# A graph attention layer on one core: the edge stage's pipeline one step deeper, its weighted sum one step later

## The chip, the core and the metric

The kernel runs on one core of a Trainium2 chip. The core has five engines with instruction queues of their own: TensorE (PE, matrix products and transposes through the PSUM banks), VectorE (DVE), ScalarE (ACT), GpSimd (POOL) and SyncE (SP, here DMA issues and bookkeeping). They wait for each other by semaphores. The metric is the device time of one execution in microseconds (us), median of several runs.

## The reference, cut to what matters

```python
h = relu(layer_norm(x))                         # x: 6250 rows of 256, float32
q, k, v = h @ wq + bq, h @ wk + bk, h @ wv + bv
scores = sum(q[dst] * k[src], -1) / 16 + (edge_weight * we + be)   # 200,000 edges
p = exp(scores - segment_max(scores, dst)[dst])
out = segment_sum(p * v[src], dst) / segment_sum(p, dst)           # softmax over each dst's edges
y = layer_norm(h + out + h @ ws + bs) * g1 + b1
result = x + layer_norm(y + gelu(y @ w1 + b_ff1) @ w2 + b_ff2) * g2 + b2
```

The edge list is sorted by `dst`, and `dst` is drawn as the whole part of 6250 u^2 with u uniform in 0 to 1. So the low rows have many edges and the high ones few: the share of the edges with dst below r is the square root of r / 6250.

## The kernel before

**Stages.** (1) Setup: x is normalised, q is multiplied with the key weights beforehand and kept as three bf16 parts (`q3`), the plan of the edge stage is worked out, the normalised rows h go to HBM (`h_rows`). (2) The edge stage, 440 steps. (3) A tail per block of 128 rows: product with wv, layer norm, feed-forward, layer norm, output.

**Edge stage.** The 200,000 edges are cut into 391 chunks of 512 (4 columns of 128 edges), padded to 392. The rows belong to 49 blocks of 128. A step is one pair of a chunk and a block; a chunk that reaches over a block's end takes one more step. A loop trip holds 8 steps (U), and a table `steps_tab`, made in setup, says which chunk and block each has.

For a chunk, GpSimd gathers the 512 source rows from HBM with four indirect DMAs of 128 rows (L488) into one of 8 slots of `rows`. Then, in a step:

- DVE marks by a one-hot table which edge has which row of the block (`mark`, L705), two steps ahead of its dot products, and ACT makes the matching mask (`prepare`, L585).
- PE expands q to the edges by 12 bf16 matmuls into banks 0 to 3, in two halves (`expand_q`, L1011).
- DVE multiplies each bank with the gathered rows and sums along them (`edge_scores`, 4 instructions L832, then L838).
- PE spreads the four columns of scores over bank 4 (`spread_scores`, L1017), DVE masks and takes the running maximum (L886), ACT takes the exponential (L618, L619), PE transposes it back (L1066), ACT copies it out of PSUM in two halves (L622).
- PE sums the gathered rows with these weights in fp32, 4 matmuls (L1079), and DVE adds the sum with its decay into `acc` (`add_sums`, L845).

In iteration s the loop does the dot products of step s + 1 and the masked maximum, exponential and weighted sum of step s; `add_sums` adds step s - 1. On PE one iteration is: transpose back, first half of the expansion of s + 2, spread of s + 1, second half, weighted sum of s. Once per trip PE also transposes a block of h (L1025) and projects it by ws (L1031, L1033), and ACT copies the results out of bank 5.

**Order and queues.** Each engine's order is written out by hand. What ties GpSimd to the rest is SP's loop over chunks: it waits until chunk c has landed (L366 to L368), tells DVE so, then waits until the weighted sum of the chunk four before it is done (L372), and gives that slot back (`slot_free`). The gather of chunk c + 4 waits for this. The first 8 chunks are gathered in setup (L478), so the ninth waits for the first weighted sum. `free_tab` holds, for each chunk, after which step its slot is free.

DVE and PE load the next trip's steps into registers once per trip (L854, L1057).

```python
used_up = sp.to_reg(sp.snap(regs[u], min_val=1, max_val=T + B + S) + r * TP)   # L369
sp.wait_ge(summed, used_up)                                                     # L372
sp.sem_inc(slot_free, 1)
```

## Time and profile before

| | us |
|---|---|
| median of 3 runs | 2334.37 (2331.2 to 2334.62) |
| span of the profiled execution | 3211.3 |
| in it: up to the first step's L886 | 143.58 |
| from there to the last step's L886 | 2804.32 |
| from there to the end | 263.40 |

The profiled execution is one execution with the hardware profiler on; its span is from its first to its last instruction, and that is all that is recorded of its time. It is 877 us above the median of the runs, more than a third, so shares of its span must not be carried over to a run as they are. Busy shares over its span: PE 76%, DVE 55%, POOL 51%, ACT 37%.

In timeline rows the columns are: start in us, length in us, engine, line, operation, out<-in, count; in brackets the idle time of the engine before it and who ended it. "issue" is time in which the engine waited for nothing that the profile shows, and "remote" a wait whose end no recorded instruction explains.

### The profile page before, as it was taken

To read this page: it belongs to the slowest core of one execution; us is meant where nothing else is said; L and a number is where in the kernel's file an instruction comes from. 1 tells how busy PE (TensorE), PEld (TensorE's weight loads), DVE (VectorE), ACT (ScalarE), POOL (GpSimd) and SP (SyncE) were. 2 spreads that over 40 slices of the span, in tenths; PEclk is the share of its full clock that TensorE was granted. 3 is DMA by queue.
4 is the path that set the end of the run, shared out by engine and by line. 5 is a ranking of instruction groups with operands and counts; after the bars stand their busy time and mean duration, and the time that the engine had idled before them with its cause. 6 is when DMAs were issued, how large, how long until landed. Compare 5 with 4: busy or idle time off the path is not lost. (4 is left out here: it accounts for less than half of the span.)

```text
span 3211.3 us, 68474 instructions
## 1 busy us (share of the span) xinstructions
PE 2427.3 (76%) x14747; PEld 1996.1 (62%) x14748; DVE 1767.6 (55%) x7372; ACT 1193.2 (37%) x2930; POOL 1635.5 (51%) x1828
## 2 busy tenths in 40 slices
PE   7577677777777777777777777777777777778998
PEld 5455556556555556565656566665666666657897
DVE  7454455555555545554555555555555555556787
ACT  6333333333333333333333333333333333334666
POOL 5355565555555545555554555555555445441154
PEclk8898899899899989998998999899988899999999
DMA  7233333333233323333233333332333233222222
GB/s 231 76 103 103 99 105 101 103 98 107 90 100 100 96 86 101 97 98 96 90 102 92 96 90 96 96 98 87 96 96 100 87 92 95 83 93 71 82 74 68
DMA packets 148148, 311.29 MB, mean 97 GB/s; under 512 B 33566, under 2 KB 84625, under 8 KB 148104
## 3 DMA queue, kind: packets, MB, share of 16 engines
q0 software_dynamic: 75264, 205.62, 21.5%
q1 hardware_dynamic: 54718, 90.19, 8.6%
q10 hardware_dynamic: 18122, 14.96, 1.5%
q8 instruction: 20, 0.33, 0.0%
q14 instruction: 24, 0.20, 0.0%
HBM read 290.21 MB, written 20.43 MB: 97 GB/s over the span
## 5 line engine op out<-in xcount | busy, mean ns | idle before, releaser
L488 POOL DMA_INDIRECT work<-h_rows,idx x1536 | 1457.3, 949 | 1339.9 <-SPq L372 956.2
L1079 PE MATMUL bank<-work 128*128 x3520 | 939.0, 412 | 24.5 <-issue 17.7
L1011 PE MATMUL bank<-q,onehot 128*128 x5304 | 804.6, 291 | 1.2 <-DVE work L832 0.7
L1079 PEld LDWEIGHTS bank<-work 128*128 128x128 f32 x3520 | 700.1, 211 | 146.8 <-issue 45.2
L886 DVE CUSTOM_DVE_ANT_0 work<-bank,work 128x512 f32<-128x512 f32 x440 | 330.5, 751 | 778.7 <-remote 476.4
L622 ACT COPY work<-bank 128x256 f32<-128x256 f32 x880 | 295.0, 376 | 1182.6 <-remote 812.8
L832 DVE SCALAR_TENSOR_TENSOR work<-bank,work 128x257 bf16<-128x257 f32 x1764 | 651.6, 425 | 143.5 <-PE bank L1011 44.2
L1017 PE MATMUL bank<-ident,work 128*128 128x128 f32 x1764 | 307.4, 302 | 500.5 <-ACT work L622 313.3
L1011 PEld LDWEIGHTS bank<-q,onehot 128*128 128x128 bf16 x5304 | 549.5, 104 | 85.4 <-issue 1.7
L1017 PEld LDWEIGHTS bank<-ident,work 128*128 128x128 f32 x1764 | 212.8, 148 | 578.0 <-ACT work L622 442.4
L1066 PE MATMUL bank<-ident,work 128*128 128x128 f32 x1760 | 283.6, 285 | 191.8 <-ACT work L619 182.8
L1066 PEld LDWEIGHTS bank<-ident,work 128*128 128x128 f32 x1760 | 214.8, 145 | 277.2 <-ACT work L619 230.6
L618 ACT ACTIVATE work<-work 128x1 f32<-128x1 f32 x440 | 129.5, 294 | 674.5 <-DVE work L886 550.3
L845 DVE SCALAR_TENSOR_TENSOR acc<-acc,work,bank 128x257 f32 x441 | 212.1, 481 | 230.4 <-remote 156.9
L619 ACT ACTIVATE work<-work 128x512 f32<-128x512 f32 x440 | 311.5, 708 | 0.0
L585 ACT ACTIVATE work<-onehot 128x512 bf16<-128x512 bf16 x442 | 282.9, 640 | 0.0
L705 DVE TENSOR_SCALAR onehot<-dst_words,node 128x512 bf16 x443 | 163.2, 368 | 72.5 <-issue 44.3
L832 DVE DVE_READ_ACCUMULATOR work<-bank,work 128x1 f32 x1764 | 145.0, 82 | 0.0
L838 DVE TENSOR_TENSOR work<-work,ew_all 128x4 f32<-128x4 f32 x441 | 72.5, 164 | 107.4 <-DVE work L832 43.5
L1405 PE MATMUL bank<-work,dst_words 128*128 128x128 f32 x784 | 96.0, 275 | 0.5 <-DVE work L1308 0.5
L1413 PE MATMUL bank<-dst_words,work 128*128 128x256 f32 x392 | 92.6, 379 | 0.0
L1405 PEld LDWEIGHTS bank<-work,dst_words 128*128 128x128 f32 x784 | 91.5, 192 | 1.2 <-issue 0.5
(195 smaller groups left out, 1519.5 us busy)
## 6 DMA issues: line engine op xcount, KB each, us to landing
dst_words<-dst_short SPq DMA_DIRECT2D x99, 512.0 KB
work<-h_rows,idx POOLq DMA_INDIRECT x1568
bias<-h_rows ACTq DMA_DIRECT2D x56, 128.0 KB
r_rows<-bias ACTq DMA_DIRECT2D x55, 128.0 KB
work<-r_rows SPq DMA_DIRECT2D x49, 128.0 KB, 2.3
h_rows<-acc SPq DMA_DIRECT2D x12, 512.0 KB, 6.6
work<-in_x SPq DMA_DIRECT2D x12, 512.0 KB, 3.5
out<-work SPq DMA_DIRECT2D x48, 128.0 KB, 1.7
```

Source lines behind the costliest of these rows:

```text
L488: pool.indirect_dma_start(rows[:, u, j, 0:D], None, h_rows, bass.IndirectOffsetOnAxis(idx[:, half, u * J + j:u * J + j + 1], 0)).then_inc( ...
L585: nc.scalar.activation(outside[:, k, :], onehot[:, k].rearrange("p j n -> p (j n)"), ACT.Copy, scale=BIG, bias=-BIG).then_inc(outside_done, 1)
L619: nc.scalar.activation(probsT, masked, ACT.Exp, bias=new_max, scale=-1.0).then_inc(exp_done, 1)
L622: nc.scalar.copy(probs[:, 2 * half:2 * half + 2, :].rearrange("p j n -> p (j n)"), banks[5 - half][:, 0:2 * P]).then_inc(probs_done, 1)
L832: last = nc.vector.scalar_tensor_tensor(out=product[:, j, 0:D1], in0=banks[j][:, 0:D1], scalar=SCALE, in1=rows[:, bass.ds(slot, 1), j, :], ...
L845: nc.vector.scalar_tensor_tensor(out=a, in0=a, scalar=decay[:, k:k + 1], in1=banks[6 + k][:, 0:D1], op0=ALU.mult, op1=ALU.add).then_inc(ad ...
L886: nc.vector.tensor_tensor_reduce(out=masked, in0=banks[4][:], in1=outside[:, k, :], scale=-1.0, scalar=old_max[:, k:k + 1], op0=ALU.add, o ...
L1011: last = nc.tensor.matmul(banks[j][:, 0:D1], onehot[:, k, j, :], q3[:, bass.ds(b, 1), c, 0:D1], start=(c == 0), stop=(c == 2))
L1017: last = nc.tensor.transpose(banks[4][:, j * P:(j + 1) * P], score[:, k, j:j + 1].broadcast_to([P, P]), ident[:])
L1066: last = nc.tensor.transpose(banks[5 - half][:, j * P:(j + 1) * P], probsT[:, (2 * half + j) * P:(2 * half + j + 1) * P], ident[:])
L1079: last = nc.tensor.matmul(banks[6 + k][:, 0:D1], probs[:, j, :], rows[:, bass.ds(slot, 1), j, :], start=(j == 2), stop=(j == 1))
L1405: last = nc.tensor.matmul(banks[2 + place(b)][:, m * P:(m + 1) * P], w1_sb[:, c, m * P:(m + 1) * P], unit_T[:, place(b), c * P:(c + 1) * P ...
```

## The change

- The dot products run two steps ahead of the maximum instead of one (two `edge_scores` before the loop, `regs[u + 2]` in it), the marks four ahead instead of three, the expansion three ahead instead of two.
- PE's iteration s is now: spread of s + 1, transpose back of s (all four columns into bank 5), the whole expansion of s + 3, then the weighted sum of step s - 1 in one piece. Iteration 0 sums a zeroed `probs`, and the last sum comes behind the loop. `summed` counts one more per step of a chunk, so each slot is given back one step later (`free_tab`, + 2 instead of + 1).
- ACT copies the weights out in one instruction of 512 columns after the next mask instead of two of 256 before it. `masked` and `probs` have two buffers, `decay` four.
- The block of h and its projection go through unused columns of banks 6 and 7 in halves of 128 columns, at u = 1 to 6 of a trip, and DVE waits for the copies in four of the eight steps.
- A step's number has the chunk in its low 15 bits and the block above, which takes shift operations out of DVE's and PE's loops.

Gathers, tail, and every product of the setup stay as they are.

```diff
+                def copy_hTe(turn, c):
+
+                    act.wait_ge(hTe_ready, turn * 2 + (c + 1))
+                    nc.scalar.copy(hT_e[:, c * P:(c + 1) * P], banks[6 + c][:, R_AT:R_AT + P]).then_inc(hTe_copied, 1)
+                    if c == DC - 1:
+                        act.dma_start(h_in, h_rows[bass.ds((turn + 1) % B * P, P), :]).then_inc(h_back, 16)
...
-                        nc.scalar.activation(decay[:, k:k + 1], old_max[:, k:k + 1], ACT.Exp, bias=new_max, scale=-1.0)
-                        nc.scalar.activation(probsT, masked, ACT.Exp, bias=new_max, scale=-1.0).then_inc(exp_done, 1)
-                        for half in (1, 0):
-                            act.wait_ge(turned, s * 2 + (2 - half))
-                            nc.scalar.copy(probs[:, 2 * half:2 * half + 2, :].rearrange("p j n -> p (j n)"), banks[5 - half][:, 0:2 * P]).then_inc(probs_done, 1)
+                        nc.scalar.activation(decay[:, u % 4:u % 4 + 1], old_max[:, k:k + 1], ACT.Exp, bias=new_max, scale=-1.0)
+                        nc.scalar.activation(probsT[:, k, :], masked[:, k, :], ACT.Exp, bias=new_max, scale=-1.0).then_inc(exp_done, 1)
                         prepare(s + 2, k)
-                        for at, body in ((3, copy_hTe), (6, copy_r), (7, store_r)):
-                            if steps == U and u == at:
-                                body(act.snap(act.to_reg(r * NW + i), min_val=0, max_val=B * NW))
+                        if steps == U and u in (2, 3):
+                            copy_hTe(act.snap(act.to_reg(r * NW + i), min_val=0, max_val=B * NW), u - 2)
+                        if steps == U and u in (5, 6):
+                            copy_r(act.snap(act.to_reg(r * NW + i), min_val=0, max_val=B * NW), 6 - u)
+                        act.wait_ge(turned, s + 1)
+                        nc.scalar.copy(probs[k][:].rearrange("p j n -> p (j n)"), banks[5][:]).then_inc(probs_done, 1)
+                        if steps == U and u == 7:
+                            store_r(act.snap(act.to_reg(r * NW + i), min_val=0, max_val=B * NW))
 
                 act.wait_ge(plan_done, 1)
                 trips(act, trip)
...
-                edge_scores(ahead[0], 0, 0, 0)
+                nc.vector.memset(probs[1], 0.0).then_inc(probs_done, 1)
+                edge_scores(ahead[0], 0, 1, 0)
                 dve.wait_ge(outside_done, 1)
                 mark(place_of_mark(ahead[2]), 0)
+                edge_scores(ahead[1], 0, 2, 1)
+                dve.wait_ge(outside_done, 2)
+                mark(place_of_mark(ahead[3]), 1)
                 dve.wait_ge(sums_set, 2)
...
 
                         dve.wait_ge(ones_set, 1)
                         dve.wait_ge(spread, step)
-                        dve.wait_ge(outside_done, step)
                         dve.wait_ge(max_read, step)
-                        nc.vector.tensor_tensor_reduce(out=masked, in0=banks[4][:], in1=outside[:, k, :], scale=-1.0, scalar=old_max[:, k:k + 1],
+                        nc.vector.tensor_tensor_reduce(out=masked[:, k, :], in0=banks[4][:], in1=outside[:, k, :], scale=-1.0, scalar=old_max[:, k:k + 1],
                                                        op0=ALU.add, op1=ALU.min, accum_out=new_max).then_inc(masked_done, 1)
-                        edge_scores(step_at(regs[u + 1]), r, s + 1, 1 - k, meanwhile)
+                        edge_scores(step_at(regs[u + 2]), r, prepared, k, meanwhile)
                         here = block_at(u)
                         dve.wait_ge(masked_done, step)
                         nc.vector.tensor_scalar(neg_max[:, bass.ds(here, 1)], new_max, 0.0, None, ALU.add).then_inc(max_kept, 1)
                         if to_next:
-                            place[0] = place_of_mark(step_at(regs[u + 3 - U]))
-                        blocks[u + 3] = place[0][2]
-                        dve.wait_ge(outside_done, after_next)
-                        mark(place[0], 1 - k)
+                            place[0] = place_of_mark(step_at(regs[u + 4 - U]))
+                            blocks[u + 1] = block_of(dve, step_at(regs[u + 1 - U]))
+                        blocks[u + 4] = place[0][2]
+                        dve.wait_ge(outside_done, prepared)
+                        mark(place[0], k)
                         read_max(s + 1, 1 - k, block_at(u + 1))
-                        add_sums(s, 1 - k, dve.snap(held, min_val=0, max_val=B) if u == 0 else blocks[u - 1])
-                    dve.reg_mov(held, dve.to_reg(blocks[steps - 1]))
+                        if steps == U and u in (2, 3):
+                            dve.wait_ge(hTe_copied, dve.to_reg((r * NW + i) * 2 + (u - 1)))
+                        if steps == U and u in (5, 6):
+                            dve.wait_ge(r_copied, dve.to_reg((r * NW + i) * 2 + (u - 2)))
+                        add_sums(s, u + 2, dve.snap(held[u], min_val=0, max_val=B) if u < 2 else blocks[u - 2])
+                    dve.reg_mov(held[0], dve.to_reg(blocks[steps - 2]))
+                    dve.reg_mov(held[1], dve.to_reg(blocks[steps - 1]))
                     dve.reg_mov(steps_done, dve.to_reg(first + steps))
 
...
+                def turn_probs(k):
+
+                    for j in range(J):
+                        last = nc.tensor.transpose(banks[5][:, j * P:(j + 1) * P], probsT[:, k, j * P:(j + 1) * P], ident[:])
+                    last.then_inc(turned, 1)
+
+                def sum_rows(k, half, slot):
+
+                    for j in (2 * half, 2 * half + 1):
+                        last = nc.tensor.matmul(banks[6 + k][:, 0:D1], probs[k][:, j, :], rows[:, bass.ds(slot, 1), j, :], start=(j == 2), stop=(j == 1))
+                    if half == 0:
+                        last.then_inc(summed, 1)
+
                 pe.wait_ge(plan_done, 1)
...
+                expand_q(1, 1, ahead[1])
                 pe.wait_ge(scored, 1)
                 spread_scores(0)
-                pe.wait_ge(dotted, 2)
-                expand_q(1, 1, ahead[1])
+                pe.wait_ge(onehot_done, S + 3)
+                pe.wait_ge(dotted[0], 2)
...
                         s, k = first + u, u % 2
-                        b, slot = block_of(pe, step_of[u + 2]), slot_of(pe, step_of[u] >> (BLOCKS.bit_length() - 1))
+                        b = block_of(pe, step_of[u + 3])
+                        pe.wait_ge(masked_done, s + 1)
+                        pe.wait_ge(scored, s + 2)
+                        spread_scores(1 - k)
                         pe.wait_ge(exp_done, s + 1)
-                        for half in (1, 0):
-                            for j in range(2):
-                                last = nc.tensor.transpose(banks[5 - half][:, j * P:(j + 1) * P], probsT[:, (2 * half + j) * P:(2 * half + j + 1) * P], ident[:])
-                            last.then_inc(turned, 1)
-                        pe.wait_ge(onehot_done, s + (S + 3))
-                        pe.wait_ge(dotted, s * 2 + 3)
-                        expand_q(k, 0, b)
-                        pe.wait_ge(scored, s + 2)
-                        pe.wait_ge(probs_done, s * 2 + 1)
-                        spread_scores(1 - k)
-                        pe.wait_ge(dotted, s * 2 + 4)
-                        expand_q(k, 1, b)
-                        for j in (2, 3, 0, 1):
-                            if j == 0:
-                                pe.wait_ge(probs_done, s * 2 + 2)
-                            last = nc.tensor.matmul(banks[6 + k][:, 0:D1], probs[:, j, :], rows[:, bass.ds(slot, 1), j, :], start=(j == 2), stop=(j == 1))
-                        last.then_inc(summed, 1)
-                        if steps == U and u == 2:
-                            turn_h(pe.snap(pe.to_reg(r * NW + i), min_val=0, max_val=B * NW))
-                        if steps == U and u == 5:
-                            project_h(pe.snap(pe.to_reg(r * NW + i), min_val=0, max_val=B * NW))
+                        pe.wait_ge(probs_done, s + 1)
+                        turn_probs(k)
+                        pe.wait_ge(onehot_done, s + (S + 4))
+                        pe.wait_ge(dotted[0], s + 3)
+                        expand_q(1 - k, 0, b)
+                        pe.wait_ge(dotted[1], s + 3)
+                        expand_q(1 - k, 1, b)
+                        sum_rows(1 - k, 1, slot)
+                        sum_rows(1 - k, 0, slot)
+                        slot = slot_of(pe, step_of[u])
+                        if steps == U and u in (1, 2):
+                            turn_h(pe.snap(pe.to_reg(r * NW + i), min_val=0, max_val=B * NW), u - 1)
+                        if steps == U and u in (4, 5):
+                            project_h(pe.snap(pe.to_reg(r * NW + i), min_val=0, max_val=B * NW), 5 - u)
+                    pe.reg_mov(slot_before, pe.to_reg(slot))
```

On PE, in the first iteration of the loop, before the change, from the spread of the next step's scores (L1017) through the second half of the expansion (L1011) to the weighted sum (L1079); `work` is the kernel's large working buffer:

```order
L1017 MATMUL bank<-ident,work 128x128 x4
L1074 REGISTER_ALU
L1011 MATMUL bank<-q,onehot 128x257 x6
L1079 ISA
L1079 MATMUL bank<-work 128x257
L1079 ISA
L1079 MATMUL bank<-work 128x257
L1078 REGISTER_ALU
L1079 ISA
L1079 MATMUL bank<-work 128x257
L1079 ISA
L1079 MATMUL bank<-work 128x257
```

And after it, in the same iteration, from the loop's register work on; L1052 is the spread, L1075 the transpose back, L1046 the expansion, L1081 the weighted sum, and the scores now lie in unused columns of `mean`:

```order
L1121 REGISTER_ALU
L1052 MATMUL bank<-ident,mean 128x128 x4
L1075 MATMUL bank<-ident,work 128x128 x4
L1126 REGISTER_ALU
L1127 REGISTER_ALU
L1046 ISA
L1046 MATMUL bank<-q,onehot 128x257
L1046 ISA
L1046 MATMUL bank<-q,onehot 128x257
L1046 ISA
L1046 MATMUL bank<-q,onehot 128x257 x10
L1081 ISA
```

The spread has moved from between the two halves of the expansion to the head of the iteration, and the sum behind the expansion is that of the step before.

On DVE, between the first marks and the first masked maximum of the loop (L886), before the change; L705 is a mark, the two TENSOR_LOADs fetch trip counts and steps:

```order
L705 ISA
L705 TENSOR_SCALAR onehot<-dst_words,node 128x512
L291 TENSOR_LOAD n_trips
L292 ISA
L903 UNCONDITIONAL_BRANCH
L904 TENSOR_LOAD steps_tab
L905 UNCONDITIONAL_BRANCH
L905 ISA
L886 ISA work<-bank,work 128x512
```

And after it, from the same mark (now L726) on; L855 are the dot products of a second step, L861 its scores:

```order
L726 TENSOR_SCALAR onehot<-dst_words,node 128x512
L325 REGISTER_ALU
L325 ISA
L855 ISA
L855 SCALAR_TENSOR_TENSOR work,mean<-bank,work 128x257
L855 ISA
L855 SCALAR_TENSOR_TENSOR norms,mean<-bank,work 128x257
L855 ISA
L855 SCALAR_TENSOR_TENSOR norms,mean<-bank,work 128x257
L855 ISA
L855 SCALAR_TENSOR_TENSOR norms,mean<-bank,work 128x257
L861 ISA
```

A second step's dot products, scores and mark have come in ahead of the loads and the loop.

## Rows read from the trace of the kernel before

**Rows 1.** Stretches: us, busy time of each engine, granted clock, DMA share, GB/s
```profile
143.58:2947.90 2804.32, 2087.74 (x12666) 1702.18 (x12667) 1479.92 (x6585) 952.79 (x2305) 1467.77 (x1584) 0.92 0.31 95
0.00:143.58 143.58, 92.61 (x460) 69.50 (x461) 85.45 (x256) 74.10 (x203) 66.80 (x96) 0.83 0.53 163
2947.90:3211.30 263.40, 246.96 (x1624) 224.37 (x1621) 202.20 (x531) 166.30 (x423) 100.90 (x148) 0.98 0.25 81
2938.30:2942.30 4.00, 4.00 (x31) 3.57 (x30) 3.39 (x16) 2.15 (x7) 0.00 (x0) 1.00 0.00 0
```
**Rows 2.** Waits of the whole span: total us, times, longest
```profile
POOL work L488 <- SPq L372: 956.2, 319, 41.9
ACT work L622 <- remote: 812.8, 246, 9.2
...
POOL work L488 <- issue: 383.8, 1217, 1.7
```
**Rows 3.** Timeline of PE in two steps near the stage's end
```profile
2941.19 0.60 PE L1066 MATMUL bank<-ident,work 128*128 128x128 f32 x4
...
2942.29 0.60 PE L1017 MATMUL bank<-ident,work 128*128 128x128 f32 x4
...
2943.39 1.90 PE L1079 MATMUL bank<-work 128*128 x8
2945.13 0.27 PE L1031 MATMUL bank<-work 128*128 128x256 bf16 x1
...
2946.11 0.60 PE L1066 MATMUL bank<-ident,work 128*128 128x128 f32 x4
```
**Rows 4.** Timeline of PE around one transpose of a block of h
```profile
1004.40 0.38 PE L1025 MATMUL bank<-ident,bias 128*128 128x128 f32 x2
...
1004.62 0.60 PE L1066 MATMUL bank<-ident,work 128*128 128x128 f32 x4
```
**Rows 5.** Timeline of DVE in the last step of a trip
```profile
1860.89 0.75 DVE L886 CUSTOM_DVE_ANT_0 work<-bank,work 128x512 f32<-128x512 f32 x1 [2.79 <-ACT work L585]
...
1864.39 0.35 DVE L705 TENSOR_SCALAR onehot<-dst_words,node 128x512 bf16 x1 [0.72 <-issue]
...
1864.83 0.48 DVE L845 SCALAR_TENSOR_TENSOR acc<-acc,work,bank 128x257 f32 x1
1865.74 0.75 DVE L886 CUSTOM_DVE_ANT_0 work<-bank,work 128x512 f32<-128x512 f32 x1 [0.43 <-issue]
```
**Rows 6.** Costliest groups: count, busy us, mean ns, idle before
```profile
L488 POOL DMA_INDIRECT work<-h_rows,idx x1536 | 1457.3, 949 | 1339.9 <-SPq L372 956.2
...
L886 DVE CUSTOM_DVE_ANT_0 work<-bank,work 128x512 f32<-128x512 f32 x440 | 330.5, 751 | 778.7 <-remote 476.4
```
**Rows 7.** Timeline of POOL at the first and the last gathers of the loop
```profile
150.45 1.01 POOL L488 DMA_INDIRECT work<-h_rows,idx  x1 [41.93 <-SPq L372]
...
2898.11 0.95 POOL L488 DMA_INDIRECT work<-h_rows,idx  x1 [0.30 <-issue]
2899.36 0.94 POOL L488 DMA_INDIRECT work<-h_rows,idx  x1 [0.30 <-issue]
...
2911.70 0.98 POOL L488 DMA_INDIRECT work<-h_rows,idx  x1 [11.17 <-SPq L372]
```
**Rows 8.** DMA issues: KB each, median us to landing
```profile
work<-r_rows SPq DMA_DIRECT2D x49, 128.0 KB, 2.3
```
**Rows 9.** Timeline of all engines from the first dot products to the first sum
```profile
138.75 0.43 DVE L832 SCALAR_TENSOR_TENSOR work<-bank,work 128x257 bf16<-128x257 f32 x1 [1.24 <-SPq L368]
...
141.03 0.35 DVE L705 TENSOR_SCALAR onehot<-dst_words,node 128x512 bf16 x1 [0.51 <-issue]
...
143.58 0.75 DVE L886 CUSTOM_DVE_ANT_0 work<-bank,work 128x512 f32<-128x512 f32 x1 [2.19 <-issue]
...
144.58 0.71 ACT L619 ACTIVATE work<-work 128x512 f32<-128x512 f32 x1
...
147.75 1.90 PE L1079 MATMUL bank<-work 128*128 x8
```

201 lines of the change are left out of this document (116 added, 85 removed).

## The prediction

> **What bounds the kernel now.** I read in this order: the stretches, to see where the time lies; the waits, to see who is idle; then single steps in the timelines, because in this case the shares mislead.
>
> The stretches [rows 1] show 143.58 us before the first masked maximum, 2804.32 us for the 439 periods up to the last one, and 263.40 us of tail. The change touches only the middle. There the profiled execution spends 6.39 us per step (2804.32 / 439). But its span of 3211.3 us is 877 us above the median of 2334.37, and the largest wait on ACT is one of 812.8 us on "remote" [rows 2], for which no recorded instruction is the reason. So the profiled execution holds time that a run does not have. If setup and tail are as in the profile, a run has 2334.4 - 143.6 - 263.4 = 1927.4 us for the 439 periods, 4.39 us each. The question is what makes it 4.39, and two accounts can be made from undisturbed rows.
>
> *TensorE's account.* In an undisturbed step [rows 3] PE goes from one transpose back (2941.19) to the next piece of other work (2945.13) in 3.94 us without a gap: 2.20 us for the transposes back, the spread and the 12 matmuls of the expansion, then 1.74 us for the weighted sum; the stretch 2938.3 to 2942.3 has PE busy 4.00 of 4.00 us at clock 1.00 [rows 1]. Once per trip comes the projection, 2946.11 - 2945.13 = 0.98 us, and the transpose of h, 1004.62 - 1004.40 = 0.22 us [rows 3, 4]. A trip is 8 x 3.94 + 1.20 = 32.72 us, 4.09 us per step. In the trip's last step DVE is late: it loads the next steps, and L886 to L886 takes 1865.74 - 1860.89 = 4.85 us [rows 5], 0.91 more than PE's 3.94. DVE's own work in that step ends at 1865.31, of which 0.72 is that wait, so without it it would need 3.70 and has 0.24 us to spare; 0.91 - 0.24 = 0.67 us per trip reach PE. That makes 4.09 + 0.08 = 4.17 us per step, and 439 steps 1831 us: 96 us less than a run takes.
>
> *GpSimd's account.* Gathers without a wait start every 1.25 us (2898.11, 2899.36 [rows 7]; 949 ns each [rows 6], the rest the gap to the next). A chunk is four of them, 5.0 us, longer than a step. In the profile POOL still waits 956.2 us for SP [rows 2], because the steps there are stretched; in a run they are not. The first gather of the loop starts at 150.45 after a wait of 41.93 us for the first weighted sum [rows 7]. Chunks 8 to 390 are 383 x 4 = 1532 gathers; the last starts at 150.45 + 1531 x 1.25 = 2064.2. A transfer of the same 128 KB lands 2.3 us after its issue [rows 8]: 2066.5. From there to the last L886 it is about 3.1 us (the 3.94 us period less about 0.83 us for L886, 751 ns [rows 6], and its readout), then the tail: 2069.6 + 263.4 = **2333.0 us**, against a median of 2334.37. I take this as the bound: TensorE's account misses by 96 us, this one by 1.4. Over most of the stage PE and DVE wait for chunks, though no row of the profile shows it.
>
> It does not hold to the end. Edges per block fall with the block number. Blocks 31 to 48 hold 391 x (1 - sqrt(3968 / 6250)) = 79.5 chunks, which make 97.5 steps. Gathering takes 397.5 us there, computing 97.5 x 4.17 = 406.6. So the last fifth is nearly even, with an excess of at most 9.1 us on the side of computing.
>
> **The change part by part.**
>
> *Loop, all engines.* PE keeps its products: the same 12, 4 and 4 and the same transposes; halves of 128 columns for the projection hold as many columns in all. DVE and ACT keep their tensor instructions per step, ACT with one copy for two. The gain can only be PE's wait. In the new order exp(s) can be ready about 2.4 us after PE starts the spread of s (0.44 for the spread, about 0.15 to be seen, 0.83 and 1.0 for the maximum and exponential) and PE wants it 3.94 + 0.44 = 4.38 us after: 2.0 us to spare, more than the 0.91 of the load. So a step falls from 4.17 to 4.09 us. Where POOL sets the pace, in the first 311 chunks, this is worth nothing, and it leaves PE and DVE 0.08 us more idle. In the last 97.5 steps it is worth 7.8 us at most, and nothing if the excess there is not paid today. The sum above gives 2333.0 without the excess and 2342.1 with all of it; the measured 2334.4 is nearer to none. I take **-4**, ends 0 and -8.
>
> *Before the loop.* DVE gets the dot products, scores and mark of a second step ahead of L886. From the first dot product at 138.75 to the mark at 141.03 is 2.28 us [rows 9], so L886 moves from 143.58 to about 145.9. The first chunk is now summed in PE's second iteration. Before, the sum (147.75, + 1.74 = 149.5) ended 5.9 us after L886. Now the second iteration starts after spread, transposes, expansion and the sum of nothing: exp at + 1.75 (144.58 + 0.71 - 143.58 [rows 9]), then 0.44 + 1.32 + 1.74 gives + 5.25; then 0.44, the exponential of the second step at about + 5.9, 0.44 + 1.32 + 1.74: + 9.4. So slot 0 comes back 2.3 + 3.5 = 5.8 us later, and with it the first of the 1532 gathers. A queue that never waits again carries this to its end. **+ 5.8**, ends + 2 (if DVE's second dot products hide behind the loads) and + 8.
>
> *Behind the last landing.* Before, the last chunk's dot products are followed by its maximum (3.1 us), then by 5.9 us to its sum: 9.0. Now one more step lies between (3.94), and the sum ends 1.75 + 0.44 + 1.32 + 1.74 + 1.74 = 7.0 us after the maximum: 14.0. **+ 5.0**, ends 0 (if computing, not landing, ends the stage) and + 6.
>
> *Slots and SP.* Each slot is given back a step later. Between the landing of a chunk and the gather into its slot lie 8 x 5.0 - 5.0 - 2.3 = 32.7 us; the new lag is three chunk paces and a sum, about 19 us. 14 us remain, so it costs 0. Behind SP's wait stand the news of the next landing and the load of the next window of marks; they are needed two steps later.
>
> *DVE's four waits per trip* for ACT's copies (u = 2, 3, 5, 6). Behind each stand `add_sums`, then the next L886, and for that wait ACT's exponential and PE's transposes. The transposes of h end with PE's iteration, so the copy ends about 0.5 us after DVE comes to it; 2.0 us of slack cover it: 0. The register work per step is less than before; it ran beside the tensor instructions: 0, at most a few us either way.
>
> Sum: -4 + 5.8 + 5.0 = + 6.8, and against the profiled execution's rows 2334.4 + 6.8 = **2341 us**.
>
> **Rivals.**
>
> *B. The stage is bound by TensorE's waits and its clock, not by gathers.* For it: the clock granted in the stage is 0.92 where PE has gaps, 1.00 where it has none [rows 1], and 4.17 / 0.95 is 4.39 too. It needs gathers that in a run start faster than every 1.25 us; nothing in the profile says so, since 949 ns recur with little spread, but a profile that stretches register work by 877 us may stretch that gap. Then closing PE's waits gives 4.09 us per step at full clock: 143.6 + 5.8 + 439 x 4.09 + 1.1 + 263.4 = 2209 us (1.1 is the later last sum, 7.0 - 5.9); with the clock kept at 0.95, 4.31 us per step and 2306. Middle 2258. It decides if gathers start every 1.17 us or faster.
> The Trainium skill (TensorE: Matmul & The Clock Gate, section "HAM oscillation - how this bites in real kernels") has waits in the loop pull the clock down again and again, and a loop without them keep it up; the trace agrees so far as 0.92 stands against 1.00. By that rule this change would come out at the low end of B.
>
> *C. DVE's new waits are not covered.* If ACT, with the exponential and the mask ahead of the copies, brings them more than 2.0 us late, PE stands. For 0.5 us in each of four steps of a trip: in the 311 chunks paced by gathers a step has 0.8 us to give and nothing shows; in the last 97.5 steps, 12.2 trips, it is 12.2 x 4 x 0.5 = 24 us, and 2341 + 4 + 24 = 2369 us. Against it: ACT is busy 37% of the span.
>
> *D. Both fillings are hidden.* If the first gather is only 2 us late and computing ends the stage, it is 2334.4 + 2 + 1.1 - 8 = 2330 us.
>
> **How the numbers follow.** GpSimd's pace with the two fillings paid: 0.57, its own range 2332 to 2351. D: 0.09. C: 0.06. B: 0.28. No change means within 0.2% (4.7 us), about what runs of this kernel can tell apart: 2329.7 to 2339.0. Faster: B and a third of D, and a little of the forecast's low end and of errors in the anchor: 0.34. No change: two thirds of D and a quarter of the forecast, 0.22. Slower: 0.44. For 8 in 10 the range must take in half of B: 2260 to 2353 leaves out 0.14 below and 0.06 above.
>
> **What would show it.** In the changed kernel's profile: PE's undisturbed period still 3.94 us; L886 to L886 over a trip's end 4.1 instead of 4.85; the first L488 at 156 instead of 150.45; gathers in a row still 1.25 us apart; in a profile less stretched, POOL's wait for SP shrinking while its gap of 0.30 stays. The forecast is wrong if the time falls below 2320: then a run's gathers are faster than the profile's, or 1.25 us was never the pace; a kernel with one gather left out per chunk would tell, since by this account it falls to TensorE's 4.17 us per step.

## The result: 0.34% slower

The changed kernel takes 2343.36 us (median of 7 runs, 2339.98 to 2344.62) against 2334.37 us before (7 runs beside them, 2331.2 to 2337.04): ratio 1.0034, 95% interval 1.0024 to 1.0045, or 9.0 us. I had forecast 2341 us, slower with a chance of 0.44. Size and sign came out. Two terms of the sum did not (the loop's and the last landing's), and their errors cancelled; at the start the new order cost what I had put, and a low clock in the profiled execution added 1.6 us that I had no term for.

Chips differ: in the runs above and in two series of experiments the kernel before takes 2334 to 2337 us, in two other series, on two other chips, 3256 to 3258, and the profiled execution of before (3211.3 us, 6.39 us per step) reads like the latter (x5_index_dma: 6.49 us per step), not like the former; all ratios below are within one chip.

The stretches of the changed kernel, cut at the first and the last masked maximum (L912, the old L886), in the columns of [rows 1]:

```profile
0.00:117.28 117.28, 89.66 (x472) 69.09 (x473) 88.17 (x268) 73.83 (x204) 66.62 (x96) 0.93 0.65 199
117.28:2079.52 1962.24, 1858.77 (x12935) 1602.61 (x12936) 1438.77 (x6586) 931.77 (x1976) 1471.43 (x1584) 0.99 0.45 136
2079.52:2342.80 263.28, 248.15 (x1637) 225.06 (x1635) 202.51 (x533) 166.46 (x422) 100.98 (x148) 0.98 0.26 81
```

Against [rows 1] this compares two chips, not two kernels: 117 us of setup where there were 144, 4.47 us per step where there were 6.39, a clock of 0.99 where it was 0.92. So the changed kernel needs another partner. It is x1_bounds below, the kernel before with only its counts and step numbers written in the new way (2332.8 us, ratio 0.9997, interval 0.9988 to 1.0006). Its stretches:

```profile
0.00:112.30 112.30, 87.92 (x460) 67.68 (x461) 84.71 (x257) 73.89 (x203) 67.44 (x96) 0.92 0.68 208
112.30:2069.28 1956.98, 1855.69 (x12666) 1586.17 (x12667) 1467.66 (x6586) 943.31 (x2305) 1471.24 (x1584) 1.00 0.46 136
2069.28:2331.20 261.92, 245.76 (x1623) 223.33 (x1621) 201.88 (x531) 166.09 (x423) 100.91 (x148) 0.98 0.27 81
```

GpSimd's timeline in the changed kernel: last gathers of the setup (L494), first and last of the loop (L504). It answers to [rows 7].

```profile
108.95 0.94 POOL L494 DMA_INDIRECT work<-h_rows,idx  x1 [0.31 <-issue]
129.17 0.94 POOL L504 DMA_INDIRECT work<-h_rows,idx  x1 [19.27 <-SPq L388]
130.42 0.94 POOL L504 DMA_INDIRECT work<-h_rows,idx  x1 [0.31 <-issue]
...
2056.29 0.23 POOL L507 COPY idx<-idx_all 128x32 int32 x1
2056.68 0.97 POOL L504 DMA_INDIRECT work<-h_rows,idx  x1 [0.16 <-issue]
2057.96 1.04 POOL L504 DMA_INDIRECT work<-h_rows,idx  x1 [0.30 <-issue]
...
2060.56 0.95 POOL L504 DMA_INDIRECT work<-h_rows,idx  x1 [0.30 <-issue]
```

The same of x1_bounds (setup L484, loop L494):

```profile
108.60 0.94 POOL L484 DMA_INDIRECT work<-h_rows,idx  x1 [0.30 <-issue]
119.06 1.01 POOL L494 DMA_INDIRECT work<-h_rows,idx  x1 [9.52 <-SPq L378]
120.38 0.95 POOL L494 DMA_INDIRECT work<-h_rows,idx  x1 [0.30 <-issue]
...
2050.32 0.95 POOL L494 DMA_INDIRECT work<-h_rows,idx  x1 [0.30 <-issue]
```

The waits of the changed kernel (total, times, longest), to be held against [rows 2]:

```profile
POOL work L504 <- issue: 438.5, 1440, 0.3
ACT work L645 <- PE bank L1075: 287.3, 401, 2.9
DVE work L855 <- SPq L384: 255.7, 192, 3.4
```

The reader is to see three things. GpSimd waits once, 19.27 us, for the first slot; no other gap between its gathers is longer than 0.31 us, which is the pause that follows every gather. VectorE waits for SyncE's news of landed chunks (255.7 us), so it is fed by the gathers. And the spans differ by 11.6 us, placed as follows:

| | x1_bounds | after | difference |
|---|---|---|---|
| first gather of the setup | 67.59 | 68.74 | + 1.15 |
| from it to VectorE's first dot product of the stage | 39.65 | 40.89 | + 1.23 |
| from there to the first masked maximum | 5.05 | 7.65 | + 2.60 |
| from there to the first gather of the loop | 6.77 | 11.89 | + 5.12 |
| from there to the last gather | 1931.25 | 1931.39 | + 0.14 |
| from there to the last masked maximum | 18.96 | 18.96 | 0 |
| from there to the end | 261.9 | 263.3 | + 1.4 |

The first two lines are no part of the change. In the twelve profiled executions below the start of the first ranges from 65.8 to 70.6 us, and on the chips where before takes 2334 to 2337 us the second is 39.05 to 42.82 us in the old order and 38.66 to 40.89 in the new one. The third line is firm: 5.05 us in all four traces of the old order on those chips, 7.65 or 7.66 in all three of the new one. It starts at these dot products, first of x1_bounds, then of the changed kernel:

```profile
107.24 0.43 DVE L837 SCALAR_TENSOR_TENSOR work<-bank,work 128x257 bf16<-128x257 f32 x1 [1.22 <-PE bank L1016]
109.63 0.43 DVE L855 SCALAR_TENSOR_TENSOR work<-bank,work 128x257 bf16<-128x257 f32 x1 [0.57 <-PE bank L1046]
```

What remains is 2.60 + 5.12 + 0.14 + 1.4 = 9.3 us, against the 9.0 of the medians. Most of it lies ahead of the first gather of the loop, and the 1536 gathers carry it to their end.

Not all of the 5.12 us is the new order. In the profiled execution TensorE was granted half its clock in the loop's first iterations, where x1_bounds and x10_three_early_copies_again (the new order, below) had it whole. It had stood idle for 1.78 us shortly before the fall, but for 1.79 us in x10 and 2.13 us in x1_bounds too. The stretches, first of the changed kernel, then of x1_bounds, then of x10:

```profile
119.20:122.50 3.30, 3.30 (x17) 2.52 (x17) 2.95 (x15) 1.51 (x4) 0.00 (x0) 0.50 0.00 0
114.00:117.40 3.40, 3.35 (x25) 2.96 (x26) 3.04 (x16) 1.63 (x5) 0.00 (x0) 1.00 0.00 0
116.60:119.90 3.30, 3.20 (x23) 2.87 (x24) 2.96 (x15) 1.52 (x5) 0.00 (x0) 1.00 0.00 0
```

and the expansion of the first iteration in the changed kernel, then in x10:

```profile
119.89 2.79 PE L1046 MATMUL bank<-q,onehot 128*128 x12
117.19 1.50 PE L1042 MATMUL bank<-q,onehot 128*128 x12
```

From the first maximum to the first gather of the loop x10 takes 10.35 us, of which 0.11 are a transpose of h that the changed kernel does later; that is 3.5 more than the 6.77 of x1_bounds. The changed kernel takes 11.89, and x4_three_after, whose clock fell there too, 11.90. So the new order costs 3.5 us here and the low clock 1.6. Whether the clock fell there in the runs without a profile is not recorded.

### The profile page after: what moved, and what is told of

Its sections match the earlier page's. It is cut to its first block and busy times, and to the rows that moved or that the text cites. A ratio compares the mean times of both kernels' runs of the same rounds, so it can differ in the third digit from the quotient of the medians.

```text
span 2342.8 us, 67076 instructions
## 1 busy us (share of the span) xinstructions
PE 2196.6 (94%) x15042; PEld 1896.8 (81%) x15043; DVE 1729.4 (74%) x7385; ACT 1172.1 (50%) x2601; POOL 1639.0 (70%) x1828
## 5 line engine op out<-in xcount | busy, mean ns | idle before, releaser
L504 POOL DMA_INDIRECT work<-h_rows,idx x1536 | 1460.9, 951 | 480.1 <-issue 438.5
L1081 PE MATMUL bank<-work 128*128 x3528 | 843.2, 381 | 0.0
L1046 PE MATMUL bank<-q,onehot 128*128 x5316 | 674.3, 275 | 84.4 <-DVE norms L855 83.0
L1081 PEld LDWEIGHTS bank<-work 128*128 128x128 f32 x3528 | 640.2, 191 | 80.7
L1046 PEld LDWEIGHTS bank<-q,onehot 128*128 128x128 bf16 x5316 | 511.5, 98 | 179.7 <-issue 107.1
L855 DVE SCALAR_TENSOR_TENSOR norms<-bank,work 128x257 bf16<-128x257 f32 x1326 | 492.7, 423 | 0.3 <-PE bank L1046 0.3
L645 ACT COPY work<-bank 128x512 f32<-128x512 f32 x440 | 258.2, 587 | 296.3 <-PE bank L1075 287.3
L855 DVE SCALAR_TENSOR_TENSOR work<-bank,work 128x257 bf16<-128x257 f32 x442 | 188.6, 427 | 266.5 <-SPq L384 255.7
L912 DVE CUSTOM_DVE_ANT_0 work<-bank,work,mean 128x512 f32<-128x512 f32 x440 | 328.4, 746 | 26.0 <-issue 26.0
L638 ACT ACTIVATE work<-work,mean 128x512 f32<-128x512 f32 x440 | 311.6, 708 | 0.0
L868 DVE SCALAR_TENSOR_TENSOR acc<-acc,mean,bank 128x257 f32 x442 | 212.8, 481 | 96.8 <-ACT bias L625 44.7
L1052 PE MATMUL bank<-ident,mean 128*128 128x128 f32 x1764 | 266.9, 274 | 17.7 <-DVE mean L912 14.2
L1075 PE MATMUL bank<-ident,work 128*128 128x128 f32 x1760 | 269.1, 276 | 3.6 <-ACT work L638 3.4
L1052 PEld LDWEIGHTS bank<-ident,mean 128*128 128x128 f32 x1764 | 205.9, 136 | 65.6 <-issue 38.9
L1075 PEld LDWEIGHTS bank<-ident,work 128*128 128x128 f32 x1760 | 201.6, 140 | 19.0 <-ACT work L638 16.7
L726 DVE TENSOR_SCALAR onehot<-dst_words,node 128x512 bf16 x444 | 167.4, 377 | 65.2 <-issue 35.0
L861 DVE TENSOR_TENSOR mean<-mean,ew_all 128x4 f32<-128x4 f32 x442 | 72.6, 164 | 79.5 <-DVE norms L855 32.5
L855 DVE DVE_READ_ACCUMULATOR norms<-bank,work 128x1 f32 x1326 | 109.3, 82 | 0.0
```

Of the source, the lines that this page charges most:

```text
L504: pool.indirect_dma_start(rows[:, u, j, 0:D], None, h_rows, bass.IndirectOffsetOnAxis(idx[:, half, u * J + j:u * J + j + 1], 0)).then_inc( ...
L638: nc.scalar.activation(probsT[:, k, :], masked[:, k, :], ACT.Exp, bias=new_max, scale=-1.0).then_inc(exp_done, 1)
L645: nc.scalar.copy(probs[k][:].rearrange("p j n -> p (j n)"), banks[5][:]).then_inc(probs_done, 1)
L726: nc.vector.tensor_scalar(onehot[:, k], dst_of[:, bass.ds(at, C)].rearrange("p (j n) -> p j n", j=J), node[:, bass.ds(b, 1)], None, ALU.is ...
L855: last = nc.vector.scalar_tensor_tensor(out=products[j][:, 0:D1], in0=banks[j][:, 0:D1], scalar=SCALE, in1=rows[:, bass.ds(slot, 1), j, :] ...
L868: nc.vector.scalar_tensor_tensor(out=a, in0=a, scalar=decay[:, u % 4:u % 4 + 1], in1=banks[6 + u % 2][:, 0:D1], op0=ALU.mult, op1=ALU.add) ...
```

## Experiments

### The new numbers alone, and the slot a step later

x1_bounds, the kernel before with:

```diff
-        return eng.snap(eng.to_reg(step & (BLOCKS - 1)), min_val=0, max_val=B)
+        return eng.snap(eng.to_reg(step >> CHUNK_BITS), min_val=0, max_val=B)
...
-        n = eng.snap(regs[0], min_val=NW, max_val=TRIPS)
+        n = not_below_zero(eng, regs[0], NW, TRIPS)
```

> The kernel before with two small parts of the change alone: a step's number has the chunk in its low 15 bits, and loaded counts are masked before they are waited on. The loop, the order and the slots are those of before. If gathers set the pace, register work is hidden: 2334 us, within 3. If register work on DVE and PE was on the path (the rival by which TensorE's waits bind), it is some us faster: 0.05 us per step would be 22 us, 2312. Its profile, if it is not stretched, should show the loop's gathers starting every 1.25 to 1.26 us without a wait for SP behind the first.

Measured: ratio 0.9997 (0.9988 to 1.0006). The register work of the change is worth nothing that can be told from 1.000, and the kernel stands in for the kernel before.

x2_slot_later is x1_bounds with each slot given back one weighted sum later:

```diff
-    used_up = sp.to_reg(not_below_zero(sp, regs[u], 1, T + B + S + 1) + r * TP)
+    used_up = sp.to_reg(not_below_zero(sp, regs[u], 1, T + B + S + 1) + r * TP + (1 if u >= LEAD else (trip + 127) >> 7))
```

> x1 with one edit: SP gives each slot back one weighted sum later, as the change does; nothing else of the change. If gathers set the pace, the first gather of the loop waits one more step (about 4 us) and every later one carries it: 2338 us, +4 against x1. If the stage is bound by TensorE's and DVE's waits, slots have 14 us to spare and this costs nothing: +0.

Measured: 2337.93 us, ratio 1.0014 (1.0005 to 1.0023), 5.1 us more than x1_bounds. In its timeline the first gather of the loop starts 12.32 us behind the first maximum (113.55), not 6.77; the last gather starts 5.8 us later than in x1_bounds:

```profile
125.87 0.95 POOL L494 DMA_INDIRECT work<-h_rows,idx  x1 [15.07 <-SPq L378]
```

I had expected 4 us, one iteration of TensorE (3.94). The trace has 5.55 because the clock was at 0.50 here as well, from 115.8 to 119.2 us, right at the start of the loop: the first iteration takes 5.66 us on TensorE (L1071 at 115.30 and 120.96), and the next one 3.95. Up to there this kernel runs the same instructions as x1_bounds, whose clock did not fall, so the fall belongs to the execution and not to the edit. A slot that returns one sum later costs its delay once, at the start, and nothing per chunk: the loop's gathers span 1930.3 us here and 1931.3 in x1_bounds.

### Three gathers per chunk

x3_three_before (on x1_bounds) and x4_three_after (on the changed kernel):

```diff
-                    for j in range(J):
+                    for j in range(J - 1):
                         pool.indirect_dma_start(rows[:, u, j, 0:D], ...
```

> x1 with three gathers per chunk in the loop instead of four; the fourth column of each slot keeps the rows of the first eight chunks, so a quarter of the rows is not the reference's. All else runs as before. If gathers set the pace, the chunk costs GpSimd 3.77 us instead of 5.03 and the stage falls to TensorE's 4.17 us per step: with setup and first maximum at 117 us as in the changed kernel's trace, 117 + 439 x 4.17 + 263 = 2211 us. If the stage is bound by waits between PE, DVE and ACT, it stays near 2334, less what the DMA traffic frees: 2310 to 2334.

> The changed kernel with three gathers per chunk in the loop, as x3. If gathers set the pace in both, this shows what the deeper pipeline is worth when they do not: 117 + 6 + 439 x 4.09 + 1 + 263 = 2183 us, 1.3% faster than x3. If the new order is no better by itself, it is as x3 or slower by its 6 us of filling: 2211 to 2217.

Measured: 2203.17 us (ratio 0.9442, 0.9428 to 0.9457) and 2198.12 us (0.9420, 0.9405 to 0.9434). A quarter of the gathers left out takes 130 and 145 us away, so in both kernels the gathers were the bound. That it is GpSimd's own pace and not the transfers fits the DMA engines' share of 0.46 in the stage. Without that bound a step takes 4.161 us in the old order and 4.140 in the new one, where I had worked out 4.17 and 4.09. x4 was to be 1.3% faster than x3 and is 0.2%. The stretch from 200 to 1800 us of each, and what TensorE's matmuls wait for in it, first x3_three_before:

```profile
200.00:1800.00 1600.00, 1586.10 (x11104) 1394.77 (x11103) 1289.30 (x5770) 826.03 (x2020) 990.66 (x1074) 1.00 0.39 120
```

```profile
PE bank L1071 <- ACT work L625: 13.9, 48, 0.3
```

then x4_three_after:

```profile
200.00:1800.00 1600.00, 1597.98 (x11409) 1412.78 (x11408) 1274.63 (x5797) 826.84 (x1740) 993.65 (x1080) 1.00 0.40 121
```

```profile
PE bank L1052 <- issue: 1.5, 6, 0.4
```

In the old order TensorE waits for ScalarE's exponential once per trip (48 times in 1600 us, 0.29 us each); in the new one it hardly waits. The starts of its first matmul of each iteration (L1071 in x3, L1052 in x4), in the mean over the trips in this stretch, say what a trip consists of:

| us per trip | x3_three_before | x4_three_after |
|---|---|---|
| 8 undisturbed iterations of 3.946 | 31.57 | 31.57 |
| the trip's end, over two iterations | 0.54 | 0.21 |
| transposes of h | 0.22 | 0.22 |
| projection of h | 0.97 | 1.11 |
| a trip | 33.30 | 33.11 |

So the new order takes away 0.33 of the 0.54 us that the trip's end, with its loads of the next step numbers, cost TensorE, and gives 0.14 back, because the projection in two halves of 128 columns takes longer than in one piece.

TensorE's timeline in x3_three_before over a trip's end:

```profile
1141.57 0.60 PE L1071 MATMUL bank<-ident,work 128*128 128x128 f32 x4
1145.97 0.66 PE L1071 MATMUL bank<-ident,work 128*128 128x128 f32 x4 [0.30 <-ACT work L625]
```

In x4_three_after over a half of the projection, an undisturbed iteration and a trip's end, then VectorE's:

```profile
1131.94 0.60 PE L1052 MATMUL bank<-ident,mean 128*128 128x128 f32 x4
...
1136.43 0.60 PE L1052 MATMUL bank<-ident,mean 128*128 128x128 f32 x4
...
1140.37 0.60 PE L1052 MATMUL bank<-ident,mean 128*128 128x128 f32 x4
...
1144.42 0.65 PE L1052 MATMUL bank<-ident,mean 128*128 128x128 f32 x4
```

```profile
1137.21 0.48 DVE L868 SCALAR_TENSOR_TENSOR acc<-acc,mean,bank 128x257 f32 x1 [1.05 <-ACT bias L625]
1137.61 0.74 DVE L912 CUSTOM_DVE_ANT_0 work<-bank,work,mean 128x512 f32<-128x512 f32 x1
...
1142.56 0.75 DVE L912 CUSTOM_DVE_ANT_0 work<-bank,work,mean 128x512 f32<-128x512 f32 x1 [0.44 <-issue]
```

Over the trip's end VectorE's maxima are 4.95 us apart, and TensorE's spreads only 4.05, where the old order's transposes back are 4.40 apart. In the new order VectorE may be late with little of it reaching TensorE, so the distance L912 to L912 no longer tells what a trip's end costs; the distance between spreads does.

### VectorE's four waits taken away

x8_three_early_copies is x4_three_after with the transposes and projections of h ahead of the transposes back, their copies in the same step, TensorE's wait for these ahead of its weighted sum, and VectorE's four waits gone. The part on the projections (the one on the transposes is alike):

```diff
                         spread_scores(1 - k)
+                        if steps == U and u in (4, 5):
+                            project_h(pe.snap(pe.to_reg(r * NW + i), min_val=0, max_val=B * NW), 5 - u)
...
+                        if steps == U and u in (4, 5):
+                            pe.wait_ge(r_copied, pe.to_reg((r * NW + i) * 2 + (u - 1)))
                         sum_rows(1 - k, 1, slot)
...
-                        if steps == U and u in (5, 6):
-                            dve.wait_ge(r_copied, dve.to_reg((r * NW + i) * 2 + (u - 2)))
```

> The changed kernel with three gathers per chunk in place of four (the fourth piece of a slot keeps old rows), 2198.1 us, in which VectorE waits in four steps of a trip for ScalarE's copy. Here TensorE does the transposes and the projection of h ahead of the transposes back instead of behind the weighted sum, ScalarE copies in the same step, TensorE waits for the copy before its weighted sum, and VectorE's four waits are gone. In the trace of the changed kernel with three gathers the steps around the two copies of r (sixth to eighth) take 4.85, 4.50 and 4.96 us, the others 3.5 to 4.05. Theory (the wait of VectorE for the copy, 0.8 us, then makes TensorE wait: rival C of the prediction is real wherever gathers do not cover it): the three steps fall to about 4.1, 2 us per trip, 55 trips, about 100 us: 2100 us; with the gathers' 391 x 3 x 1.258 = 1475 us no bound, TensorE's 4.09 per step gives 115 + 439 x 4.09 + 263 = 2174 as the lowest that the projections allow, so between 2150 and 2180. Rival (the last step is long because of the load of the next step numbers): the eighth step stays at 4.9, total 2190 or more.

Measured: 2686.7 us, on a chip where before takes 3257.81 (ratio 0.8245, 0.8215 to 0.8275); nothing follows for the question. Run again:

> The same kernel as x8_three_early_copies: the changed kernel with three gathers per chunk, and VectorE's four waits per trip for ScalarE's copies gone (projection ahead of the transposes back, copy in the same step). On a chip on which the kernel before takes 2334 us. Theory: the sixth to eighth step of a trip fall from 4.85, 4.50 and 4.96 us towards 4.1, the total from 2198 us to between 2150 and 2180. On the slow chip the fastest steps of each place in the trip (tenth percentile) were already 3.4 to 3.8 us and 4.57 for the eighth, so the eighth, where the next step numbers are loaded, may keep 0.5 us more than the others. Rival (the load alone makes these steps long): 2190 or more. If before is near 3258 us here too, only the order of the two says something: the ratio should stay under 0.83.

Measured: 2197.64 us, ratio 0.9407 (0.9393 to 0.9422), no different from x4_three_after's 0.9420. My theory, 2150 to 2180 us, was wrong. VectorE's waits in x4_three_after:

```profile
DVE acc L868 <- ACT bias L625: 114.9, 110, 1.1
DVE acc L868 <- ACT bias L616: 43.2, 103, 0.6
```

and in x10_three_early_copies_again, nearly the same sum in another place:

```profile
DVE work L855 <- PE bank L1042: 158.7, 258, 1.0
```

The 158 us that VectorE waited for the copies were mostly time for which it would else have waited for TensorE. TensorE is busy 1598 of 1600 us in both. From the first to the last maximum it is 1817.5 us with the four waits and 1814.9 without, so they cost at most 2.6 us even where gathers do not cover them: TensorE does.

### What makes a gather slower than 1.25 us

Start to start, gathers of the loop take 1.2581 us in x1_bounds, not 1.25, which is 12 us over 1535 of them. Some 4 us of it are GpSimd's 48 copies of indices, behind which a gather starts 1.338 us after the last one instead of 1.256; some 6 us are 78 gathers that last about 0.08 us longer than the others. x5_index_dma lets SyncE bring the indices:

```diff
+                            if u == G - 1:
+                                sp.dma_start(idx[:, bass.ds(trip & 1, 1), :], idx_all[:, bass.ds((i + 2) % NW * (G * J), G * J)]).then_inc(idx_in, 16)
...
-                    nc.gpsimd.tensor_copy(idx[:, half, :], idx_all[:, first]).then_inc(idx_set, 1)
```

> The kernel before (in the form with masked counts and the new step numbers), with GpSimd's 48 copies of the next 32 gather indices taken off GpSimd: SyncE brings them by a DMA when the eighth chunk of a trip has landed. In the trace of the kernel before in this form a gather that follows such a copy starts 1.330 us behind the last one, the others 1.256. Theory (the time is the number of gathers times their pace, behind the first one of the loop): 48 x 0.074 = 3.6 us go, 2332.8 - 3.6 = 2329.2 us, ratio to before 0.998. Rival (the computing engines are as slow as the gathers, so that a faster GpSimd is not felt): 2332.8, ratio 1.000.

Measured: 3270.89 us beside 3257.81 of before, ratio 1.0029 (1.0 to 1.0059), on one of the two slow chips. Run again:

> The same kernel as x5_index_dma, on another chip: the four runs of that series, and the kernel before beside them, took 3240 to 3280 us, where loops spend 6.4 us per step whatever is gathered when, and the idle time of GpSimd was a wait for SyncE. There a shorter gather series cannot be felt (ratio 1.003 was measured). Theory, for a chip on which the kernel before takes 2334 us: the 48 long gaps behind the index copies (1.330 us in place of 1.256) go, 3.6 us, ratio to before 0.998. Rival: ratio 1.000. If this chip is like the last one (before near 3258 us), the run says nothing on either.

Measured: 2332.81 us beside 2337.26, ratio 0.9982 (0.9973 to 0.9991), as expected. The pace is 1.2549 us in its trace, and its gathers in the loop span 1926.2 us for 1931.3. This version is faster than both kernels, by 0.2% and 0.5%.

x6_mark_other_form tests the lengthened gathers. In x1_bounds 78 of 1536 take over 980 ns instead of 946, and 77 of them start while VectorE's mark (353 ns, L710) runs; of 1093 gathers that no mark overlaps none is lengthened.

```diff
-  nc.vector.tensor_scalar(onehot[:, k], marks, of, None, ALU.is_equal)
+  nc.vector.scalar_tensor_tensor(out=onehot[:, k], in0=marks, scalar=of, in1=rows[:, 0, 0:1, D:D1].to_broadcast((P, J, P)), op0=ALU.is_equal, op1=ALU.mult)
```

> The kernel before in the same form, with VectorE's mark in the loop as a scalar_tensor_tensor (compare, then times a column of ones) in place of the tensor_scalar of 353 ns. In the traces so far 78 to 85 of 1536 gathers take 1000 to 1070 ns instead of 946, and all of them start while the 353 ns mark runs. Theory (the mark in its fast form keeps GpSimd from a port of the memory): hardly any gather is lengthened, 80 x 0.09 = 7 us go, 2332.8 - 7 = 2326 us, ratio 0.997; VectorE needs about 0.2 us more per step, which 4.46 - 4.16 = 0.30 us of room per step cover. Rival 1 (the lengthening has another cause and stays): 2333 us, ratio 1.000. Rival 2 (the longer mark makes VectorE the bound): slower than 2333, 2340 or more.

Measured on the same slow chip as x5_index_dma: 3227.3 us, ratio 0.9909 (0.9877 to 0.994). The gathers (groups: count, busy us, mean ns) of x5_index_dma:

```profile
L497 POOL DMA_INDIRECT work<-h_rows,idx x1536 | 1457.1, 949 | 1398.2 <-SPq L381 1007.9
```

and of x6_mark_other_form, with its mark:

```profile
L494 POOL DMA_INDIRECT work<-h_rows,idx x1536 | 1505.8, 980 | 1302.3 <-SPq L378 910.1
...
L714 DVE SCALAR_TENSOR_TENSOR onehot<-dst_words,node,work 128x512 bf16<-128x512 f32 x441 | 332.5, 754 | 61.5 <-issue 33.5
```

The link between mark and gather holds, and my reading of it was wrong. The other form lasts 754 ns and lengthens more gathers: 215 over 980 ns instead of 20, by 31 ns in the mean over all. Of the 252 gathers that start while it runs 206 are lengthened, and the mean of the 252 is 1141 ns; of the 265 already running when it starts none. So it is not the fast form alone that holds GpSimd up.

The traces say more than that gathers are lengthened. Of the gathers that start while a mark runs, those that start in its first 0.1 us are not lengthened in either form. Each of the others that is lengthened ends later by what was left of the mark at its start less 0.13 us (0.128 in the median of x6_mark_other_form, 0.129 in x1_bounds, eight in ten within 0.005): with 0.57 us left in x6 it is 0.45 us longer, with 0.23 us left in x1_bounds 0.10. So in both forms GpSimd stands until the mark has ended. The Trainium skill (SBUF — State Buffer, section "Who interferes with whom") has the later of the two engines blocked until the instruction of the earlier is over, and names as holders the two-port modes, and instructions with two inputs in SBUF where GpSimd reads. The traces agree with its first half; that the gather reads as well would be what the second form shows. Why this kernel is nevertheless 0.9% faster than before on that chip stays open.

x7_both has both edits:

> Both edits of the two kernels above at once, on the kernel before in the same form. Theory: they add up, 1532 gathers at 1.2505 us instead of 1.258 us: 3.6 + 7 = 11 us go, 2322 us, ratio 0.995. Rival (one hides the other, or the computing engines are the bound by then): 2326 us or more. This is also the version that is meant to be faster than both kernels.

Measured on the same chip: 3251.28 us, ratio 0.9974 (0.9944 to 1.0005). With the same long mark it shows the same 980 ns per gather, so the mark's share of the gain that I had summed was not there to be had.

### The way to the first maximum

In x1_bounds VectorE's timeline from the first mark to the first maximum:

```profile
109.43 0.35 DVE L710 TENSOR_SCALAR onehot<-dst_words,node 128x512 bf16 x1 [0.41 <-issue]
112.30 0.75 DVE L891 CUSTOM_DVE_ANT_0 work<-bank,work 128x512 f32<-128x512 f32 x1 [2.51 <-issue]
```

The 2.51 us are two loads of numbers and their register work. Two kernels move these loads ahead, into the setup; x11_index_dma_early_loads in x9's kernel, x12_after_early_loads in the changed one:

```diff
-                    dve.load(regs[0:4], steps_tab[0:1, 0:4])
+                    numbers[:] = counts(dve)
+                    dve.load(regs, steps_tab[0:1, 0:AHEAD])
```

> The kernel of x9_index_dma_again (the kernel before in the form with masked counts and new step numbers, next indices by a DMA of SyncE), and in it VectorE loads the numbers of trips and the step numbers of the first trip while the projections are still made, not between its first mark and its first masked maximum. In the trace of x1_bounds these two loads and their register work stand between the mark that starts at 109.47 and the maximum that starts at 112.30, and the engine does nothing else in 2.5 us. Theory (gathers in a row carry any shift of the first one to the end): the first gather of the loop comes 2.0 to 2.4 us earlier and the whole kernel as much: ratio to before 0.9982 - 0.0009 = 0.9972, about 2329 where before is 2335. Rival (TensorE or ScalarE is not ready earlier, or the earlier loads push the projections back by as much): 0.9982 again. This is the version meant to be faster than both kernels.

> The changed kernel with the same move alone: VectorE's loads of the numbers of trips and of the first step numbers stand in the projections, not ahead of the first masked maximum. Its own ratio to before is 1.0034. Theory (the changed kernel's loss is the later first gather of the loop, and whatever brings that gather forward comes back one for one): 2.0 to 2.4 us earlier, ratio 1.0025. Rival (its loss comes from the loop or the end of the stage): the gather comes earlier, the time stays at 1.0034.

Both fell on a slow chip (before 3256.23 us): 3273.74 us, ratio 1.0058 (1.0026 to 1.0090), and 3099.12 us, ratio 0.9550 (0.9511 to 0.9588). Whether the times come down at 2334 us was not measured. But the two traces show that little would come back. The maximum does start 2.1 us sooner behind the first dot product (2.94 us in x11, 5.54 in x12, for 5.05 and 7.65), and the first gather of the loop only 0.4 to 0.5 us sooner (x11: 11.30 us behind the first dot product, for 11.82 in x1_bounds and in x5_index_dma; x12: 17.49, for the 17.9 of the new order at full clock). What comes last is now TensorE's own start of the loop, in x11:

```profile
148.05 0.65 PE L1076 MATMUL bank<-ident,work 128*128 128x128 f32 x4 [1.66 <-issue]
```

So the 2.0 to 2.4 us of both theories were wrong and the rival (TensorE is not ready earlier) right, and the one-for-one claim rests on x2_slot_later and the table above.

x12 shows something else: on such a chip the new order is 4.5% faster than before, and x11, the old order with the same loads moved, is 0.6% slower. The waits there, of x5_index_dma (old order):

```profile
POOL work L497 <- SPq L381: 1007.9, 317, 45.8
ACT work L631 <- remote: 712.1, 211, 9.4
...
DVE work L894 <- remote: 512.3, 101, 7.8
```

and of x12_after_early_loads (new order):

```profile
POOL work L504 <- SPq L388: 828.9, 283, 55.2
ACT work L645 <- remote: 486.7, 112, 9.1
```

GpSimd has to wait for slots there, so the gathers are not the bound. My reading is that the handovers between engines are, and that an order with one more step between engines loses less by them; no run tests it.

## Why the prediction was right, and where it was not

**The bound: right.** Gathers behind each other without a wait set the time: GpSimd waits for SyncE once in the changed kernel, and the kernel that I had named as the test, with a gather left out, falls to 4.161 us per step where TensorE's account said 4.17 (a trip's end costs TensorE 0.54 us there, not the 0.67 I had put).

**The anchor of 2333.0 us: right by luck, by errors that cancel.** It took the first gather of the loop from the profile, 150.45 [rows 7]; in x1_bounds it is at 119.06, 31 us earlier. Against that the gathers take 1.2581 us each and not 1.25, + 12 us; there are 1536 of them, as [rows 6] says, where I had counted 1532 (the padded chunk 391 is gathered too), + 5; and from the last gather to the last maximum there are 18.96 us and not the 2.3 + 3.1 I had put, + 14: five maxima are still to come when the last gather starts. With a tail of 261.9 for 263.4 the errors sum to - 2, and 2333.0 - 2 is the 2331 of the span. I had seen that the profiled execution held 877 us too many, and placed all of them in the loop; 31 of them lay ahead of it. An agreement of 1.4 us was too good a reason to trust the sum.

**Loop, - 4: failed, it is 0.** A step without the gathers' bound falls by 0.02 us, not 0.08. Of the 0.67 us per trip that I gave to VectorE's load, TensorE lost 0.54, and the new order still loses 0.21 of it, where I had nothing left. And I had the projection in halves for nothing, because it has as many columns; it takes 0.14 us more per trip. Over 97.5 steps the 0.02 us are 2 us at most, and in the table they are not to be seen. L912 to L912 over a trip's end was forecast at 4.1 and is 4.95, of which 0.21 us per trip reach TensorE.

**Before the loop, + 5.8: right, and a low clock on top.** The second dot products, scores and mark measure 2.60 us; I had 2.28, because I had read up to the start of the mark and left its own length out. The later slot costs 3.5 us in x10_three_early_copies_again, as forecast. Together 6.1 us. The other 1.6 of the 7.7 us in the traces of the changed kernel are the fall of the clock at the loop's start, which the sum has no term for and which x2_slot_later had too, without the new order.

**Behind the last landing, + 5.0: failed, + 1.4.** Computing, not the landing, ends the stage in both kernels, the end 0 of my range; only the last sum comes later (8.84 us behind the last maximum for 7.48), for which I had 1.1. The errors of + 4 in the loop, + 1.9 before it and - 3.6 behind it make + 9.1 us of the sum's + 6.8; the medians of the runs show + 9.0.

**Slots, SyncE, register work, 0: right** (x1_bounds 0.9997; + 0.14 us over 1535 gathers). **VectorE's four waits, 0: right**, and more so than I thought: without the gathers too, x10 leaves rival C 2.6 us at most over the whole stage.

**Rival B** needed gathers faster than 1.17 us; they take 1.258. Its clock was that of the other chip: 1.00 in the stage of x1_bounds and 0.99 in the changed kernel, where [rows 1] had 0.92. The Trainium skill's rule (TensorE: Matmul & The Clock Gate, section "HAM oscillation - how this bites in real kernels") that waits inside the loop pull the clock down again and again agrees with before's profile, with waits of TensorE up to 6.9 us and 450 of the stage's 2804 us at the lower level. In x1_bounds, whose stage has TensorE's waits too (93 us in all, the longest 2.6), it hardly shows: 17 of 1957 us. So the 0.92 went with the chip, and the change had no clock to win. **Rival D** was half true: the end is hidden, the start is not.

## What to carry over

In a stage fed by one queue that never waits, ask of each edit only whether it moves the first entry or the pace of the queue. Whatever moves the first entry costs its full length once. A deeper pipeline is such an edit; here only the chips on which GpSimd waited for slots paid it back. And compare the profiled span with the runs first: if it is far longer, as here by 877 us, take durations of instructions from it, but no starting time and no wait. Measure a loop's period on the engine that is busy throughout, by its starts.

## What the runs showed of the hardware

- The same kernel takes 2334 to 2337 us on some chips and 3256 to 3258 us on others. Instructions of GpSimd and VectorE last as long on both (gathers 949 and 951 ns, the maximum 751 and 750); the time lies between them. From 160 to 1900 us none of SyncE's 1605 register instructions takes more than 0.4 us in x1_bounds; in x5_index_dma 118 of 1227 do, mostly 0.7 us, and in the profile of before 53 of 526. Ahead of the gathers (first one at 67.6 and 68.7) and in the tail there is no difference. What causes it was not settled; with three gathers per chunk it shrinks from 938 us (x5 against x9) to 489 (x8 against x10), though those are two different orders of work.
- A gather of 128 rows holds GpSimd for 946 ns and starts 1.25 us behind the last one at the earliest (1.245 in x1_bounds).
- A gather that starts more than 0.1 us after VectorE's mark is held until the mark ends, in both forms of the mark: it is longer by what is left of the mark less 0.13 us. One that starts earlier in the mark, or is already running, is not (but for one of 261 in x1_bounds, by 0.04 us).
- Two executions of the same instructions differ in the clock: x1_bounds kept 1.00 where x2_slot_later was granted 0.50 from 115.8 to 119.2 us, and that made the loop's first iteration 5.66 us long for 4.05.
